# Expert stage of a transformer layer on one Trainium2 core: the second product interleaved with the next tile's first, relu kept in PSUM

## What is computed

```python
probs = jax.nn.sigmoid(flat @ router_w.T)
scores, idx = jax.lax.top_k(probs, TOPK)          # TOPK = 2
h = jnp.maximum(jnp.einsum('td,edh->teh', flat, ew1) + eb1[None, :, :], 0.0)
eo = jnp.einsum('teh,eho->teo', h, ew2) + eb2[None, :, :]
routed = jnp.einsum('teo,te->to', eo, comb)
```

## Time and profile before

| | us |
|---|---|
| Time, median of 3 executions | 1530.94 |
| Lowest and highest of them | 1525.81, 1532.79 |
| Profiled execution: span from first to last instruction | 1646.1 |
| In it: first matmul of the expert stage | 906.4 |
| In it: last output sum of the expert stage starts | 1506.15 |

### The profile page before, as it was taken

The page is one execution under the profiler, slowest core; times in us unless marked ns, Lnnn a source line. Parts: engine busy times, 40 slices in busy tenths (PEclk is TensorE's granted clock), DMA queues, the critical chain, the costliest instruction groups (busy, mean ns, idle before and its releaser), DMA issues. The chain is left out here.

```text
span 1646.1 us, 31319 instructions
## 1 busy us (share of the span) xinstructions
PE 1399.0 (85%) x9849; PEld 1050.4 (64%) x9920; DVE 1197.8 (73%) x2480; ACT 983.0 (60%) x2014; POOL 545.8 (33%) x532
## 2 busy tenths in 40 slices
PE   4899999999999986991198999999999999997486
PEld 2444444444444435891198888888888888886475
DVE  3888878878888855860065888888888888885467
ACT  4688878878888875850044545545545545543355
POOL 5222222212221003547500433433433433443542
PEclk7999999999999997995599899999999999998697
DMA  7000000000000214113200655555555555550332
GB/s 307 1 2 27 2 28 9 20 28 2 27 2 14 65 39 154 39 51 129 83 0 26 207 164 197 176 168 192 176 175 186 177 179 180 181 164 31 94 106 90
DMA packets 106408, 160.42 MB, mean 97 GB/s; under 512 B 12928, under 2 KB 85888, under 8 KB 105152
## 3 DMA queue, kind: packets, MB, share of 16 engines
q1 hardware_dynamic: 97040, 132.10, 24.6%
q0 software_dynamic: 9264, 27.01, 4.9%
HBM read 121.86 MB, written 37.22 MB: 97 GB/s over the span
## 5 line engine op out<-in xcount | busy, mean ns | idle before, releaser
L470 DVE TENSOR_REDUCE att_mx<-att_psA 128x1 f32<-128x512 f32 x512 | 339.1, 683 | 57.9 <-PE att_psA L269 55.6
L387 ACT ACTIVATE att_prob<-att_psB 128x512 f32<-128x512 f32 x512 | 290.1, 603 | 79.9 <-PE att_psB L279 67.5
L1431 ACT ACTIVATE exp_h<-exp_psU,ew_b 128x256 f32<-128x256 f32 x312 | 146.8, 470 | 277.6 <-PE exp_psU L1389 210.6
L1401 PE MATMUL exp_psD<-exp_w2h,exp_hh 128*128 128x256 f32 x624 | 215.3, 345 | 50.1 <-DVE exp_hl L1466 43.5
L1462 DVE CAST exp_hh<-exp_h 128x256 fp32r<-128x256 f32 x312 | 209.1, 670 | 38.2 <-ACT exp_h L1431 33.2
L269 PE MATMUL att_psA<-att_qk 96*128 96x512 bf16 x512 | 195.8, 384 | 8.3 <-DVE att_mx L470 4.8
L1401 PEld LDWEIGHTS exp_psD<-exp_w2h,exp_hh 128*128 128x128 f32 x624 | 132.7, 213 | 90.1 <-DVE exp_hl L1466 89.3
L1402 PE MATMUL exp_psD<-exp_w2l,exp_hh 128*128 128x256 f32 x624 | 190.0, 304 | 0.0
L1403 PE MATMUL exp_psD<-exp_w2h,exp_hl 128*128 128x256 f32 x624 | 189.6, 304 | 0.0
L1466 DVE TENSOR_TENSOR exp_hl<-exp_h,exp_hh 128x256 fp32r<-128x256 f32 x312 | 173.5, 556 | 10.8
L1387 PE MATMUL exp_psU<-exp_xh,exp_w1h 128*128 128x256 f32 x624 | 177.8, 285 | 2.1 <-DVE exp_w1l L1457 2.1
(11 more groups left out here) (187 smaller groups left out, 3338.0 us busy)
## 6 DMA issues: line engine op xcount, KB each, us to landing
ew_w<-ew SPq DMA_DIRECT2D x40, 1024.0 KB
exp_w<-ew SPq DMA_DIRECT2D x38, 1024.0 KB, 6.0
exp_xs<-slots_x SPq DMA_DIRECT2D x39, 256.0 KB, 3.9
slots_y<-exp_ys POOLq DMA_DIRECT2D x39, 256.0 KB, 4.3
slots_x<-pre_acc SPq DMA_DIRECT2D x9, 1024.0 KB, 14.9
ew_b<-eb SPq DMA_DIRECT2D x39, 128.0 KB, 3.5
att_xt<-xT SPq DMA_DIRECT2D x8, 512.0 KB, 4.6
attn_rows<-att_ob SPq DMA_DIRECT2D x8, 512.0 KB, 3.2
```

The lines of the kernel that those rows point to most:

```text
L387: act.activation(prob[:, n % PR, :], psB[n % 2][:, :], ACT.Exp, scale=SCALE).then_inc(s_exp, 1)
L470: dve.reduce_max(mx[:, g % 2, n % U:n % U + 1], psA[A_BANK[n % U]][:, :], AX_X).then_inc(s_max, 1)
L1401: pe.matmul(ps, hh[:, h, rows], w2h[:, h, :], start=(h == 0), stop=False)
```

## The change

TensorE's order becomes one of periods. In period n it does, for each of the 8 hidden columns in turn, the six second-product matmuls of tile n (`down`, both row halves) and the six first-product matmuls of tile n+1 (`up`); after column 1 it turns the rows of tile n+2. The other engines follow the same periods, with `up` for tile n+1 and `ahead` for tile n+2.

- `h32` is gone. ACT writes relu back into PSUM in place, DVE makes `hh` and `hl` from there, two hidden columns (512 elements) at a time. `psU` is now four banks of two columns, `psD` two banks for even and odd tiles.
- ACT does four groups in a period: two relus of tile n+1, a piece of `w1h` of tile n+2, a piece of `w2h` of tile n+1; after the second pair of relus also `xh` of tile n+2.
- Pieces 0 to 2 of `w1l` stay on DVE, piece 3 goes to GpSimd with a semaphore of its own, `s_w1p`, behind its four pieces of `w2l`.
- The output sum is one instruction of 512 columns, and the store moves from GpSimd's queue to SP's, which handles it five steps late. `b2` has its own semaphore.
- SP's step t issues, in this order: the store of tile t-5, b2 of tile t-3, the rows and w1 of tile t, then b1 and w2 of tile t-1. Before w1 of tile t it waits until the low parts of w1 of tile t-2 are done, on both engines.

The semaphore `s_w1` still counts w1 and b1 together, and `w1_hi` still waits for both.

```diff
--- before.py
+++ after.py
@@ class ExpertWeights @@
+        self.s_b2 = [a.sem(f"b2_loaded{i}") for i in range(2)]
...
-        sp.dma_start(self.b2[:, k, :], self.sources[3][bass.ds(e, 1), :].to_broadcast([P, self.b2.shape[2]])).then_inc(self.s_w2[k], 16)
+        sp.dma_start(self.b2[:, k, :], self.sources[3][bass.ds(e, 1), :].to_broadcast([P, self.b2.shape[2]])).then_inc(self.s_b2[k], 16)
@@ experts @@
-    WP = 4
-    HP = HC // WP
-    assert NL % 2 == 1 and RT * D == 512 and RT == 2
+    WP = HC // 2
+    VECTOR_W1 = 3
+    assert NL % 2 == 1 and RT * D == 512 and DC * LT == 512
...
-        h32 = a.sb("h32", [P, 4, LT], F32)
...
-        psT = a.ps("psT", [P, 512], F32)
-        psU = [a.ps(f"psU{i}", [P, 512], F32) for i in range(4)]
-        psD = [a.ps(f"psD{i}", [P, 512], F32) for i in range(RT)]
+        psT = a.ps("psT", [P, DC, LT], F32)
+        psU = [a.ps(f"psU{i}", [P, 2, LT], F32) for i in range(WP)]
+        psD = [a.ps(f"psD{i}", [P, RT, D], F32) for i in range(2)]
...
@@ sync: the old tile() is printed with the kernel @@
+            def step(t):
+                late, out, was = t.plus(-1), t.plus(-3), t.plus(-5)
+                if was.exists():
+                    was.wait(sp, s_y, 1, 1)
+                    store(was)
+                if out.exists() and not (out.it is None and out.n == 0):
+                    out.wait(sp, s_y, 1, -1)
+                    weights.load_b2(sp, out.k, expert_of(out))
+                if t.exists():
+                    t.wait(sp, s_tr, 1, -1)
+                    sp.dma_start(xs[:, t.k], x_tile[bass.ds(t.j, 1)].rearrange("o p r d -> p (o r) d")).then_inc(s_x[t.k], 16)
+                    if not (t.it is None and t.n == 0):
+                        t.wait(sp, s_w1l, VECTOR_W1, -VECTOR_W1)
+                        t.wait(sp, s_w1p, WP - VECTOR_W1, VECTOR_W1 - WP)
+                        weights.load_w1(sp, t.k, expert_of(t))
+                if late.exists() and not (late.it is None and late.n == 0):
+                    e = expert_of(late)
+                    late.wait(sp, s_rel, HC, -HC)
+                    weights.load_b1(sp, late.k, e)
+                    late.wait(sp, s_w2l, WP, -WP)
+                    weights.load_w2(sp, late.k, e)
+
+            for n in range(5):
+                step(Tile(n))
+            with sp.Fori(0, (NL - 5) // 2) as it:
+                for n in (5, 6):
+                    step(Tile(n, it))
+            for n in range(NL, NL + 5):
+                step(Tile(n))
...
+        def periods(eng, period):
+
+            for n in range(-1, LOOP[0]):
+                period(Tile(n))
+            with eng.Fori(0, (LOOP[1] - LOOP[0]) // 2) as it:
+                for n in range(LOOP[0], LOOP[0] + 2):
+                    period(Tile(n, it))
+            for n in range(LOOP[1], NL):
+                period(Tile(n))
@@ gpsimd @@
+            def w1_lo(t, q):
+                t.wait(pool, s_w1h, WP, q + 1)
+                pool.tensor_tensor(w1_piece(w1l, q), w1_piece(w1[t.k], q), w1_piece(w1h, q).bitcast(F32),
+                                   ALU.subtract).then_inc(s_w1p, 1)
+
+            def w2_lo(t, q):
+                t.wait(pool, s_w2h, WP, q + 1)
+                pool.tensor_tensor(w2_piece(w2l, q), w2_piece(w2[t.k], q), w2_piece(w2h, q).bitcast(F32),
+                                   ALU.subtract).then_inc(s_w2l, 1)
+
+            def period(t):
+                up, ahead = t.plus(1), t.plus(2)
                 for q in range(WP):
...
+                    if up.exists():
+                        w2_lo(up, q)
+                if ahead.exists():
+                    for q in range(VECTOR_W1, WP):
+                        w1_lo(ahead, q)
@@ tensor @@
+            def down(t, h):
+                if h == 0:
+                    t.wait(pe, s_y, 1, -1)
+                if h % 2 == 0:
+                    t.wait(pe, s_hl, WP, h // 2 + 1)
+                    t.wait(pe, s_w2l, WP, h // 2 + 1)
                 for r in range(RT):
...
+                    ps, rows = psD[t.k][:, r, :], slice(r * P, (r + 1) * P)
+                    pe.matmul(ps, hh[:, h, rows], w2h[:, h, :], start=(h == 0 and r == 0), stop=False, skip_group_check=True)
+                    pe.matmul(ps, hh[:, h, rows], w2l[:, h, :], start=False, stop=False, skip_group_check=True)
+                    ins = pe.matmul(ps, hl[:, h, rows], w2h[:, h, :], start=False, stop=(h == HC - 1), skip_group_check=True)
+                if h == HC - 1:
+                    ins.then_inc(s_dn, 1)
+            def up(t, h):
+                if h == 0:
+                    t.wait(pe, s_xl, 1, 1)
+                if h % 2 == 0:
+                    q = h // 2
+                    if q < VECTOR_W1:
+                        t.wait(pe, s_w1l, VECTOR_W1, q + 1)
+                    else:
+                        t.wait(pe, s_w1p, WP - VECTOR_W1, q - VECTOR_W1 + 1)
+                    t.wait(pe, s_hl, WP, q + 1 - WP)
+                ps, cols = psU[h // 2][:, h % 2, :], slice(h * P, (h + 1) * P)
...
+            def period(t):
+                nxt, ahead = t.plus(1), t.plus(2)
                 for h in range(HC):
...
+                    if t.exists():
+                        down(t, h)
+                    if nxt.exists():
+                        up(nxt, h)
+                    if h == 1 and ahead.exists():
+                        turn(ahead)
@@ scalar @@
-                    t.wait_pair(act, s_w1, 32, 32)
...
+                    t.wait_pair(act, s_w1, 32, 1)
...
+            def relu(t, q):
+                t.wait(act, s_up, HC, 2 * q + 2)
+                for i in range(2):
+                    h = 2 * q + i
+                    act.activation(psU[q][:, i, :], psU[q][:, i, :], ACT.Relu, bias=b1[:, t.k, h:h + 1]).then_inc(s_rel, 1)
+            def period(t):
+                up, ahead = t.plus(1), t.plus(2)
+                for q in range(WP):
+                    if up.exists():
+                        relu(up, q)
+                    if q == 1 and ahead.exists():
+                        rows_hi(ahead)
+                    if ahead.exists():
+                        w1_hi(ahead, q)
+                    if up.exists():
+                        w2_hi(up, q)
@@ vector @@
+            def hidden_hi(t, q):
+                t.wait(dve, s_rel, HC, 2 * q + 2)
+                dve.tensor_copy(hh[:, 2 * q:2 * q + 2, :], psU[q][:, :, :]).then_inc(s_hh, 1)
+
+            def hidden_lo(t, q):
+                t.wait(dve, s_hh, WP, q + 1)
+                dve.tensor_tensor(hl[:, 2 * q:2 * q + 2, :], psU[q][:, :, :], hh[:, 2 * q:2 * q + 2, :].bitcast(F32),
+                                  ALU.subtract).then_inc(s_hl, 1)
+
+            def output(t):
+                t.wait_pair(dve, s_b2, 16, 1)
+                t.wait_pair(dve, s_st, 16, 0)
+                t.wait(dve, s_dn, 1, 1)
+                dve.tensor_tensor(ys[:, t.k], psD[t.k][:, :, :], b2[:, t.k, :].unsqueeze(1).to_broadcast([P, RT, D]),
+                                  ALU.add).then_inc(s_y, 1)
+
+            def period(t):
+                was, up, ahead = t.plus(-1), t.plus(1), t.plus(2)
+                for q in range(WP):
+                    if up.exists():
+                        hidden_hi(up, q)
+                    if q == 0 and was.exists():
+                        output(was)
+                    if 1 <= q <= VECTOR_W1 and ahead.exists():
+                        w1_lo(ahead, q - 1)
+                    if up.exists():
+                        hidden_lo(up, q)
+                    if q == 1 and ahead.exists():
+                        rows_lo(ahead)
```

More of the change, by code:

```diff
@@ L1299, in wait_pair @@
                 else:
+                    assert v > 0
                     eng.wait_ge(s[self.k], v + self.it * per_use)
[L1302 to L1318, removed]
         block = ctx.enter_context(nc.Block())
@@ L1323, in _ @@
         def _(sp):
[L1324 to L1339, removed]
@@ L1348, in _ @@
                                base=0, pattern=[[-1, P]], channel_multiplier=1).then_inc(s_id, 1)
-            def store(k, j):
-                pool.dma_start(y_tile[bass.ds(j, 1)].rearrange("o p r d -> p (o r) d"), ys[:, k]).then_inc(s_st[k], 16)
-            def tile(t):
-                for q in range(WP):
[L1356 to L1364, removed]
+            def w1_lo(t, q):
[8 more added lines that the diff above has]
+                up, ahead = t.plus(1), t.plus(2)
+                for q in range(WP):
+                    if up.exists():
[3 more added lines that the diff above has]
+                        w1_lo(ahead, q)
+            for q in range(VECTOR_W1, WP):
+                w1_lo(Tile(0), q)
+            periods(pool, period)
         @block.tensor
@@ L1370, in turn @@
             def turn(t):
-                t.wait_pair(pe, s_x, 16, 16)
+                t.wait_pair(pe, s_x, 16, 1)
                 t.wait(pe, s_xl, 1, 0)
-                for r in range(RT):
[L1374 to L1380, removed]
-                for h in range(HC):
```

(39 more changed lines are left out.)

86 lines of the change are left out of this document (37 added, 49 removed).

## The result

| | Time, us (median; lowest and highest) | Against the kernel before |
|---|---|---|
| Predicted | 1613 (1580 to 1660) | slower |
| Measured | 1548.33 (1544.13 to 1553.08), before 1530.44 | 1.0116 times, 95% interval 1.0087 to 1.0144 |
| Again, second set of runs | 1547.37, before 1529.74 | 1.0119 times, 1.0102 to 1.0136 |

The changed kernel is 18 us slower, 1.2%.

A forecast was written before the change was run, and what follows sets the result against it. The prediction took a serial loop through b1's load to bound the kernel: 7.6 + 3.1 + 0.8 + 6.1 + 0.1 = 17.7 us a tile, 36 times, made the stage 82 us longer: 1530.9 + 82 = 1613 us, range 1580 to 1660.

The forecast's parts named there:

- The ring: Expert-stage loop through ScalarE, GpSimd, SP and the w1/b1 transfer, nothing overlapping: 17.7 us a tile, against 15.4 before.
- GpSimd's tail: After ScalarE's last w2h cast, GpSimd's two last subtractions, w2l then w1l, slowed by VectorE: 3.1 us.
- outside the ring: Claim that TensorE does not set the period: ScalarE wants its last up 5.6 us after the up matmuls end.
- the stage's two ends: Expert stage before and after the 36 repeats: start at 908.5, then from 1545.7 to the last second product at 1587.8.
- the turn: One period of the ring, one tile of the expert stage: 17.7 us, ends 16.3 and 19.0, repeated 36 times.
- term 4: From w1's issue on SP to b1's landing, taken from the stage's first step: 6.1 us, bounds 5.4 and 7.1.
- term 1: ScalarE from b1's landing to its last w2h piece, with six relus at 0.46: 7.6 us, bounds 7.0 to 8.2.
- SP, with signals: SP reads the expert's number before issuing w1, 0.8 us, with 0.1 for signals.
- the low ends: Rival: all terms of the ring at their low bounds together, about 16.3 us a tile, 1563 us; chance 5%.
- b1 does not overtake w1: Denies the rival that b1's 4 KB does not queue behind w1's 1 MB: ring 14.4 us, 1494 us; chance 7%.
- TensorE did not join the ring: Denies the rival that TensorE's half clock holds a whole period: 22 us a tile, 1768 us; chance 8%.
- the 5 us on which the prediction leaned: Claim that every half-clock stretch of TensorE in the expert stage ends within some 5 us.

The follow-up runs named there:

- the first experiment: Changed kernel with b1 given a semaphore of its own, awaited by a tile's first relu: 1508.99 us beside 1638.86 before, 0.9203 times; 1393.07 beside 1528.11 on another chip.
- The last experiment: Changed kernel with two already met waits for each relu in place of one for a pair: 1545.69 us beside 1528.11 for the kernel before.

## Why the prediction was right in direction and wrong in size

**Right.** The order of loads, not an engine, sets the pace, and what the engines allow is 12.0 us a tile: the first experiment shows 11.94. The ring runs through b1, w1's wait and GpSimd's tail, and four experiments moved it, each through the term that was touched (to 13.0, 16.96, 17.2 and 20.1 us). TensorE was outside the ring, VectorE's work was 309.1/39 = 7.9 us a tile where I had at most 9.0, and the stage's two ends together are within 2 us of the forecast: its sum was too high by 82 - 22.7 = 59 us (22.7 is what the stage grew by in the first two profiles), and 36 x 1.6 = 57 of them lie in the turn itself.

The direction had little to spare. A turn shorter by another 0.5 us, 18 us in 36 turns, would have made the kernel no slower than before.

**Wrong: the length of the turn, 16.1 where the sum said 17.7.** The steps that failed are term 4, from w1's issue to b1's landing, and term 1, ScalarE's share, both taken too long. By the terms as the prediction numbered them (measured values are means over the turns):

| Term | Forecast | Measured, changed kernel | What was wrong |
|---|---|---|---|
| 1. ScalarE | 7.6 | 6.94 | the relu step, 0.46 in place of 0.36, six times |
| 2. GpSimd's tail | 3.1 | 2.82 | VectorE held its `w2l` piece by 0.23 (1.50 against 1.27); the `w1l` piece took 1.29 |
| 3. SP, with signals | 0.9 | 0.92 | |
| 4. w1 issued to ScalarE going on | 6.1 | 5.4 (5.2 in most turns) | the row chosen |
| Sum | 17.7 | 16.1 | |

Term 4 missed by 0.7 us a turn in the mean, 25 us in all, and by 0.9 in most turns. I took the stage's first step. There w1 was issued about one microsecond behind two loads of rows. In the ring nothing has been issued on SP's queue for 11 us when w1 is (997.75 and 1008.78 above). The landing times of the changed kernel, from the views of L1201 (w1) and L1204 (b1):

```profile
DMA to landing us min/median/max: 4.8/5.0/5.4
...
DMA to landing us min/median/max: 1.6/4.0/8.1
```

w1 lands in 5.0 us, not 5.3, and b1 about 0.3 behind it, not 0.8 (902.51 + 5.5 against 901.95 + 5.3). That the rows in front made the first step longer fits this, but no run tests it. I had a nearer row, w2's 5.4, and used it only as a bound. In five of the 36 turns the term was 6.2 to 6.7 us; in a second profile of the same kernel, in one. What delays those is open.

Term 1 missed by as much, 0.7 us a turn, 0.6 of it in the relus. The last experiment and the row above show why: a step measured between two instructions held a wait that the view doesn't name. The estimate from the Trainium skill's table (VectorE: DVE Perf Modes, the errata section), 0.36 us, is the step that was measured: 0.72 for two. The Trainium skill's page ScalarE: Activation LUTs, section on the activation pipeline, says that PSUM is the faster destination. The trace does not bear that out for the step: with SBUF two relus took 0.71.

Two things made the range too narrow. The first is a slip in adding up: the low ends are 7.0 + 2.8 + 0.8 + 5.4 + 0.1 = 16.1, not 16.3, and the high ends 19.7, not 19.0. By its own bounds the prediction reached down to 16.1, the turn that was measured, and to 1613 - 36 x 1.6 = 1555 us. The second is that terms 1, 2 and 4 all came out at or near their low ends (6.94 against 7.0, 2.82 against 2.8, 5.4 against 5.4), to which together I gave 5%. Each bound was drawn around the row I had picked, so the misses were not independent.

**The rivals.** b1 does not overtake w1: it stood 4.05 us behind its issue with 1 MB in front, 1.57 with none. TensorE did not join the ring: in every turn ScalarE's wait ends with b1. Its clock was 0.91 in the stage. But its stretches at half clock were longer than the 5 us on which the prediction leaned: from 839 to 846 the granted clock was 0.53.

**Best version.** b1 moved or freed gives 1393 us, 9% below the kernel before. relu in PSUM is not what pays there: it empties VectorE (389 to 273 of 400 us) and moves no time while TensorE is the bound; with the ring kept it is worth 36 us. The gain lies in the rest of the change. No run takes that apart into the interleaving, VectorE's wider instructions and the `w1l` piece on GpSimd; that the interleaving does most of it is likely, since it is what took TensorE's 89.3 us of waits for `hl` away, but not shown.

## What to carry to other kernels

Before costing the engines of a new schedule, follow each load from the count that its user waits for to the place of its issue: a small load that shares a semaphore with a large one, issued behind a wait on the period's last instruction, made a ring here, with ScalarE, GpSimd, SP and the transfer in series, 155 us of a stage of 622. Price each term of such a ring from a row in the same state (an empty queue, no producer near), and check a step between two starts against the producer's end. Add up the low ends and the high ends as carefully as the middle. And where a sum of terms is repeated 36 times, a tenth of a microsecond in a term is 4 us in the result.

## What was not expected of the hardware

- No cast from PSUM was held up, though 153 of the 156 ran beside a subtraction of GpSimd's, while casts of the same 512 columns from SBUF were. The line view of the cast gives ns as min/median/max, first for the changed kernel, then for the one with relu in SBUF and the ring kept:

```profile
L1509 DVE CAST exp_hh<-exp_psU x156: 679/691/695, 832.9 to 1445.8; 128x512 fp32r<-128x512 f32 x156
```

```profile
L1510 DVE CAST exp_hh<-exp_h x156: 409/885/1527, 831.4 to 1477.2; 128x512 fp32r<-128x512 f32 x156
```

- A transfer of 4 KB issued 1.3 us behind one of 1 MB was late by 2.4 us (median landing 4.0 against 1.6); behind 2 MB (7.6), by 6.0.
- The same program takes 1530 us on one chip and 1639 on another, with an expert stage of the same length (467.7 and 468.4 us for the one kernel profiled on both kinds; 598.9 and 599.7 for the kernel before, on the slower kind alone).
